# A GRU scan step: z and 1 - z as two sigmoids in place of one tanh and two copies

## What is computed

```python
xz = einsum('btd,de->bte', seq, W_z)   # and xr, xh alike, for all tokens at once
def step(h, xs):
    xzt, xrt, xht = xs
    z = sigmoid(xzt + h @ U_z + vz)
    r = sigmoid(xrt + h @ U_r + vr)
    hh = tanh(xht + r * h @ U + vh)
    h_new = (1.0 - z) * h + z * hh
    return (h_new, h_new)
```

## Time and profile before

| what | value |
|---|---|
| median of 3 runs | 6809.69 us (6809.19 to 6810.33) |
| the profiled execution's own time | 6811.76 us |
| its span in the trace | 6809.9 us |
| busy: PE, DVE, ACT | 5998.4, 4955.6, 3331.6 us |
| TensorE clock granted, mean | 0.996 of full speed |

### The profile page before, as it was taken

One profiled execution on the slowest core, in us unless ns is written; L12 is line 12 of the kernel. 1 busy time (PEld: TensorE's weight loads), 2 busy tenths in 40 slices (PEclk: granted clock), 3 DMA queues, 4 the chain that ended last, 5 costly groups with the idle time before them and its releaser, 6 DMA issues.

```text
span 6809.9 us, 488240 instructions
## 1 busy us (share of the span) xinstructions
PE 5998.4 (88%) x200232; PEld 5642.2 (83%) x200232; DVE 4955.6 (73%) x43503; ACT 3331.6 (49%) x22603; POOL 3.5 (0%) x13
## 2 busy tenths in 40 slices
PE   7888888888888888888888888888888888888888
PEld 7888888888888888888888888888888888888888
DVE  5777777777777777777777777777777777777777
ACT  3444444444444444444444444444444444444444
POOL 0000000000000000000000000000000000000000
PEclk8999999999999999999999999999999999999999
DMA  2000000000000000000000000000000000000000
GB/s 84 17 18 15 18 17 18 17 17 17 18 17 18 15 18 17 18 18 15 18 17 18 17 18 15 18 17 18 17 17 17 18 17 18 15 18 18 17 18 15
DMA packets 80315, 129.97 MB, mean 19 GB/s; under 512 B 12336, under 2 KB 18480, under 8 KB 80304
## 3 DMA queue, kind: packets, MB, share of 16 engines
q1 hardware_dynamic: 80304, 129.81, 5.5%
HBM read 20.46 MB, written 8.65 MB: 4 GB/s over the span
## 4 chain that ended last, share of the span: by engine, by line
PE 71%; DVE 26%; issue 3%; SPq 0%; DMA 0%; ACT 0%; ACTq 0%; DVEq 0%
PE pair_r L252 30%; PE ps_z L252 24%; PE pair_h L252 17%; DVE pair_h L487 8%; DVE h_part L522 5%; DVE h_part L541 4%; DVE h_part L527 2%; DVE keep L523 2%; DVE zn L536 2%; DVE h_part L532 2%; PE ps_z L212 0%; DMA u_raw<-in_L_cond_U 0%; PE ps_o L212 0%; DVE u_max L424 0%; PE ps_x L224 0%
## 5 line engine op out<-in xcount | busy, mean ns | idle before, releaser
L252 PEld LDWEIGHTS pair_r<-h_part,u_part 128*128 128x128 f16 x65536 | 1845.1, 96 | 1119.9 <-DVE h_part L541 1115.8
L252 PE MATMUL pair_r<-h_part,u_part 128*128 128x32 f16 x65536 | 2048.7, 177 | 771.1 <-DVE h_part L541 758.6
L252 PE MATMUL pair_h<-rh_part,u_part 128*128 128x32 f16 x65536 | 2016.6, 177 | 12.5 <-DVE rh_part L505 12.5
L252 PE MATMUL ps_z<-h_part,u_part 128*128 128x32 f16 x65536 | 1961.5, 176 | 0.0
L252 PEld LDWEIGHTS pair_h<-rh_part,u_part 128*128 128x128 f16 x65536 | 1842.8, 96 | 17.3 <-DVE rh_part L505 15.7
L252 PEld LDWEIGHTS ps_z<-h_part,u_part 128*128 128x128 f16 x65536 | 1795.3, 95 | 0.0
L487 DVE TENSOR_REDUCE pair_r<-pair_r 128x4 f32<-128x20 f32 x4096 | 759.4, 186 | 818.1 <-PE pair_r L252 615.1
L351 ACT ACTIVATE pair_r<-pair_r 128x4 f32<-128x4 f32 x4096 | 644.8, 158 | 1445.1 <-DVE pair_r L487 1182.4
L487 DVE TENSOR_REDUCE pair_h<-pair_h 128x4 f32<-128x12 f32 x4096 | 717.7, 175 | 665.7 <-PE pair_h L252 665.7
L351 ACT ACTIVATE th_z<-ps_z 128x8 f32<-128x8 f32 x2048 | 364.1, 178 | 1046.0 <-DVE ps_z L487 1046.0
L337 ACT ACTIVATE pair_h<-xp 128x8 f32 (+1 forms) x2049 | 369.9, 181 | 807.8 <-DVE zn L536 807.8
(11 more groups left out here) (70 smaller groups left out, 3275.9 us busy)
## 6 DMA issues: line engine op xcount, KB each, us to landing
w_stage<-w_in SPq DMA_DIRECT2D x384, 256.0 KB, 2.3
x_tok<-in_x SPq DMA_DIRECT2D x68, 128.0 KB, 2.6
out_dram<-o_tok SPq DMA_DIRECT2D x66, 128.0 KB, 2.3
mlp_w<-in_L_cond_W SPq DMA_DIRECT2D x2, 1024.0 KB, 6.9
u_raw<-in_L_cond_U_r SPq DMA_DIRECT2D x1, 1024.0 KB, 5.6
u_raw<-in_L_cond_U_z SPq DMA_DIRECT2D x1, 1024.0 KB, 7.6
u_raw<-in_L_cond_U SPq DMA_DIRECT2D x1, 1024.0 KB, 10.3
w_in<-in_L_cond_W_r SPq DMA_DIRECT2D x4, 256.0 KB, 9.8
```

Of the source, the lines that this page charges most:

```text
L252: last = nc.tensor.matmul(bank[:, SLOT * m:SLOT * m + WIDE].rearrange("p (r n) -> p r n", n=n), u_part[:, g, part, k, gm * P:(gm + 1) * P] ...
```

## The change

z_keep and z_mul are each computed by a Sigmoid activation straight from the sums in `ps_z`: z from the sum, and 1 - z from the sum with the sign of the scale turned. `th_z`, its semaphore and the two copies go. z_mul is now z and no longer z times 2^13, so the factor H_SCALE moves into the two products with the candidate on VectorE, which become SCALAR_TENSOR_TENSOR. Both sigmoids stand ahead of the seed of `pair_r`. A fourth scale (the negative one) is computed once and loaded once into a register. tanh is still used for r and for the candidate.

```diff
+        act_scale = sb("act_scale", [P, G + 1])
-        th_z = sb("th_z", [P, S])
...
-            for g in range(G):
-                act.reg_load(scale_reg[g], tanh_scale[0:1, g:g + 1].bitcast(I32))
+            for g in range(G + 1):
+                act.reg_load(scale_reg[g], act_scale[0:1, g:g + 1].bitcast(I32))
...
                     A(hist[:, prv, :], h_cur[:, :], ACT.Copy)
-                    tanh(th_z[:, :], ps_z, Z, S, "z_sum", t1, "z_th")
-
+                    act.wait_ge(s["z_sum"], t1)
+                    A(z_keep[:, :], ps_z[:, SUM:SUM + S], ACT.Sigmoid, scale=scale_reg[G]).then_inc(s["z_keep"], 1)
+                    A(z_mul[:, :], ps_z[:, SUM:SUM + S], ACT.Sigmoid, scale=scale_reg[Z]).then_inc(s["z_ok"], 1)
                     seed(pair_r, R, nxt)
-                    act.wait_ge(s["z_th"], t1)
-                    A(z_keep[:, :], th_z[:, :], ACT.Copy, scale=-0.5, bias=0.5).then_inc(s["z_keep"], 1)
-                    A(z_mul[:, :], th_z[:, :], ACT.Copy, scale=H_SCALE / 2, bias=H_SCALE / 2)
                     tanh(ps_h[0][:, TANH:TANH + HS], ps_h[0], H, HS, "h0_sum", t1, "h0_th")
...
+            V.tensor_scalar(act_scale[:, G:G + 1], u_pow[:, Z:Z + 1], -2.0 ** -27, None, ALU.mult)
...
                 def new_high(hf):
                     dve.wait_ge(s[f"h{hf}_th"], t1)
-                    V.tensor_tensor(h_part[:, kc[hf], NEW, :], kb(z_mul[:, half[hf]]),
-                                    kb(ps_h[hf][:, TANH:TANH + HS]), ALU.mult)
+                    V.scalar_tensor_tensor(h_part[:, kc[hf], NEW, :], kb(z_mul[:, half[hf]]), H_SCALE,
+                                           kb(ps_h[hf][:, TANH:TANH + HS]), ALU.mult, ALU.mult)
 
                 def new_full(hf):
-                    V.tensor_tensor(zn[:, half[hf]], z_mul[:, half[hf]], ps_h[hf][:, TANH:TANH + HS],
-                                    ALU.mult).then_inc(s[f"zn{hf}"], 1)
+                    V.scalar_tensor_tensor(zn[:, half[hf]], z_mul[:, half[hf]], H_SCALE, ps_h[hf][:, TANH:TANH + HS],
+                                           ALU.mult, ALU.mult).then_inc(s[f"zn{hf}"], 1)
```

More of the change, by code:

```diff
@@ L77, in gru_kernel @@
         pre_scale = sb("pre_scale", [P, G])
-        tanh_scale = sb("tanh_scale", [P, G])
+        act_scale = sb("act_scale", [P, G + 1])
         x_tok = sb("x_tok", [P, D])
@@ L112, in gru_kernel @@
                  "x_in x_tr y_ok y_copied proj0_mm proj0_ok wst_in proj_mm o_sum o_tr o_ev out_st "
-                 "seed0 h0_ready r0_mm r1_mm z_mm z_keep h_ok h0_mm h1_mm r0_sum r1_sum z_sum h0_sum h1_sum r0_th r1_th z_th h0_th h1_th "
+                 "seed0 h0_ready r0_mm r1_mm z_mm z_keep h_ok h0_mm h1_mm r0_sum r1_sum z_sum h0_sum h1_sum r0_th r1_th z_ok h0_th h1_th "
                  "rh32_0 rh32_1 rh0 rh1 keep_ok zn0 zn1 hs0 hs1 copied")
@@ L342, in _ @@
                 seed(banks, g, 0).then_inc(s["seed0"], 1)
-            scale_reg = [act.alloc_register(f"tanh_scale_{g}") for g in range(G)]
-            for g in range(G):
-                act.reg_load(scale_reg[g], tanh_scale[0:1, g:g + 1].bitcast(I32))
+            scale_reg = [act.alloc_register(f"act_scale_{g}") for g in range(G + 1)]
+            for g in range(G + 1):
+                act.reg_load(scale_reg[g], act_scale[0:1, g:g + 1].bitcast(I32))
             def tanh(to, bank, g, n, wait, t1, done):
@@ L436, in _ @@
             for g in range(G):
-                V.tensor_scalar(tanh_scale[:, g:g + 1], u_pow[:, g:g + 1], 2.0 ** -28, None, ALU.mult)
+                V.tensor_scalar(act_scale[:, g:g + 1], u_pow[:, g:g + 1], 2.0 ** (-27 if g == Z else -28), None, ALU.mult)
+            V.tensor_scalar(act_scale[:, G:G + 1], u_pow[:, Z:Z + 1], -2.0 ** -27, None, ALU.mult)
             dve.wait_ge(s["upow"], 3)
```

## The result

The changed kernel takes 6847.35 us (median of 4 runs, 6845.31 to 6849.56) against 6809.89 before, now the median of 4 runs. The ratio is 1.0055, with a 95% interval of 1.0040 to 1.0069: slower by 37 us. The span of the profiled execution is 6843.2 us.

What follows compares the result with a forecast made beforehand. Each step was taken as bound by the ring of h products, sum, tanh, new state and next r products. Step terms of -4 us plus 53 for table loads gave +49 on 6809.7, so 6859 us, range 6825 to 6910.

Steps and rivals of the forecast that it cites:

- the ring: The loop of each step taken to bound the kernel: h products, sum, tanh, new state, next r products.
- the loads decide: Two table loads per outer loop pass, 1.283 us each, were to lose 1.65 us a block, +53 us over 32 blocks.
- The first load: Ahead of a block's first r tanh: h products 1.0 us late each block, with slack of only 0.01.
- The second load: Behind the hist copy, ahead of z_keep: tanh of the first half late, 0.65 us lost a block, least 0.55.
- The z arc: In every step z_keep is ready 0.24 us earlier, so L532 isn't pushed: gain 0.00 to 0.02 us, taken as 0.01.
- The factor in the products: VectorE's candidate products L532 and L536 become SCALAR_TENSOR_TENSOR: cost 0 to 0.012 us a step, taken as 0.008.
- signs of being wrong: Wrong if a load waits, its next activation starts much after its end, or steps without loads change over 0.02 us.
- The other two signs: A load held back behind a wait, or the first activation behind a load starting much after its end.
- The block distance: Time from one block to the next, 210.2 us before, was to become 211.8.
- The rival of a switch that costs twice the load's row: The activation behind each load waits 1.28 us more, both fully on the path: 6941 us, chance 0.09.
- The rival of a faster ring: Early z_keep shortens the step between the first half's sum and L541 by 0.04 us: 6781 us, chance 0.04.
- The rival of a load at every change of function: Two table loads in each step, over 1.2 us x 2048, more than 2500 us: above 9300 us, chance 0.02.

## Why the prediction was right, and where it was off

I predicted 6859 us with a range of 6825 to 6910 and slower with 0.9; it came to 6847, slower, 12 us below. Direction and main mechanism held: the loads stall the ring once a block. Of the sizes only the first load's was good; two errors of 12 and 16 us in the small terms nearly cancelled, which was luck. By its steps:

*That the loads decide:* shown. With the set loaded ahead the sign turns (0.9984).

*The first load, 1.0 us a block with no slack behind it:* shown, 1.03. My bounds for how late the tanh would be were 0.71 and 1.31; the trace gave 0.37 of branch before the load, which makes 1.05.

*The second load, 0.65:* wrong in size, measured 0.28, about half of what I had called the least, 0.55. Two parts of that sum failed. I let the hist copy end 0.9 to 1.0 later than before; but when the r tanh is late, ScalarE's queue closes up. From the r tanh's start to the end of hist it took 0.74 in the earlier trace rows, and 0.34 after the change (285.67 to 286.01), so the load began 0.4 us earlier in relation to the delayed ring than I had it. And I took 0.12 between starts for the activations behind the load; it was 0.07 from z_keep to z_mul (287.31, 287.38) and 0.23 from z_keep to the tanh, not 0.36. This overstated the sum by 12 us.

*The z arc, a gain of 0.00 to 0.02 a step, taken at 0.01:* right in place, too large in sum. 12 steps of 64 gain 0.023, the others nothing, 9 us in all where 0.01 in each of 2048 steps is 20. Of the two steps read, the one with the late L532 was a fifth step, and I let it count for half of all. The run with the seed moved shows that the early start of z_keep does it, and that neither the sigmoids nor the dropped copy is needed.

*The factor in the products, 0.008 a step:* measured nothing (0.9987 without, 0.9984 with), where I had 16 us. Net, the steps outside the loads gave -9 us where I had -4: 12 us too much gain against 16 us of a cost that isn't there.

*The clock:* not in the prediction at all. The stall takes it to 0.50 for 3.4 or 6.8 us a block, which costs about 3 us in all by the traces.

So the terms read 32 x (1.03 + 0.28 + 0.1) - 9 = 36 us against 37 measured and 49 predicted.

One of my signs of being wrong did come: steps without a load were to change by no more than 0.02 us, and the fifth steps changed by 0.023 and the third step of a block by 0.083. The first is the z arc, gathered in few steps, the second the clock. The other two signs did not come: the loads started without a wait, and the activations right behind them. The block distance came to 211.4 (211.8 expected), TensorE's wait for the gated state to 40.0 us (45), and L521 follows the first half's sum by 0.087 (0.08).

The rival of a switch that costs twice the load's row is refuted: in the block shown the r tanh starts 0.01 behind the load and z_keep 0.02 (287.29 to 287.31 as rounded; 0.011 to 0.012 in all 64 cases), and of the 1033.6 us that ScalarE idled before z_keep, all but 0.4 were waits for the z sum. The Trainium skill, ScalarE: Activation LUTs, section What ACT_TABLE_LOAD costs, gives 1283 ns, which all 65 loads show, and 1380 ns of drain on top, of which the activations behind these loads show nothing. The rival of a faster ring would have needed 0.033 us a step, and the ring gave 0.023 in one step of five. The rival of a load at every change of function is refuted by the 65 loads; its price was also misworked, since one load of 1.283 us in each of 2048 steps is 2628 us and two are 5255.

Left open: how the clock's fall depends on the length and place of the stall. A gap of 0.93 us brought it in all of the last 31 blocks, one of 0.82 in 22, one of 0.23 in 11, and the usual gap of 0.3 to 0.6 us a step alone in none. Open too is why the fifth step's seed starts later, which is read from the code alone.

## What to carry to other kernels

Before using a second activation function in a loop, look in the built program for table loads, at loop heads above all. Here two loads stood in each pass although one set serves both functions; one throwaway sigmoid before the loop took both out and was worth 0.7%. My reading, which no run shows by itself, is that the set that comes in from outside and the one that comes round from the loop's end have to agree there. Ask also which part of a change brings its gain: moving one seed behind z_keep gave all that the sigmoids gave, with no table to load. And when a late engine catches up, its queue closes up, so the second delay is smaller than the first one carried along.

## What the runs showed of the hardware that I had not expected

The granted clock of TensorE fell to 0.50 in 11 of 31 blocks after one extra gap of 0.23 us in a stream that already idles 0.3 to 0.6 us a step; the stretches at 0.50 lasted 3.4 us, and behind gaps of 0.93 us now and then 6.8. At 0.50 the r, z and h products (128 x 32) ran almost as fast, 1.05 against 1.00 us for 32 of them, while four 128 x 128 fp32 transposes took 1.09 against 0.64. An ordinary activation lets the next one start 0.10 us before its end (284.68 against 284.78); behind a table load the next one starts 0.011 us after it. The work of 0.64 us put in the gap kept the clock at 1.00 in 28 of 31 blocks; the same work moved there from behind the gap did so in two.
